# Writing each image's output inside the next image's filter, in four transfers, and asking for the second half of the pixels in the attention's tail

## What is computed

```
q_in = jnp.quantile(x.reshape(B, C, -1), 0.5, axis=-1)        # median of each channel
x = x + relu(-q_in)[:, :, None, None]
y = upfirdn2d(x, lpf, up=2, ...); y = maximum(y, 0); x = upfirdn2d(y, lpf, down=2, ...)
...
spec = rfft2(x); gate = sigmoid(w2 @ gelu(w1 @ abs(spec)))
xf = x + irfft2(spec * gate)
q = xf @ q_w + q_b;  k, v = two strided convolutions of xf, layer norm, projections (320 keys)
out = softmax(q k / 4) v;  out = out @ proj_w + proj_b + x
```

## Time and profile before

| | |
|---|---|
| median of 3 runs | 12392.25 us (12376.9 to 12396.04) |
| profiled execution's own time | 12365.55 us |
| its span, first to last instruction | 12364.0 us |
| mean granted TensorE clock | 0.912 |
| TensorE / VectorE / ScalarE / GpSimd busy | 86% / 72% / 59% / 22% |
| prologue, until the first pass's first TensorE instruction | 257.4 us |
| distance of the 4 MB writes of successive passes, mean of 15 | 756.65 us |

### The profile page before, as it was taken

How to read it: one execution, slowest core, us unless ns; L and a number is a source line. 1 busy time by engine, 2 the same in 40 slices (tenths; PEclk the granted TensorE clock), 3 DMA queues, 4 the chain that set the end, 5 groups by cost and what they waited for, 6 DMA issues and landing times. The chain is left out here.

```text
span 12364.0 us, 195989 instructions
## 1 busy us (share of the span) xinstructions
PE 10662.7 (86%) x71137; PEld 5494.3 (44%) x71137; DVE 8876.6 (72%) x15501; ACT 7240.1 (59%) x12109; POOL 2719.0 (22%) x4368
## 2 busy tenths in 40 slices
PE   2898898989989799898988989889898898979989
PEld 1544435344353443535435354443534435344353
DVE  6777677776677777767677677767777667777776
ACT  5556465664646646466564665646566464664646
POOL 1212213122131221312213121221312213122130
PEclk9899898988989899898998989989898898989989
DMA  1021220212212022130211202112021221202213
GB/s 47 19 48 40 44 60 25 52 29 49 56 29 55 22 52 52 31 71 10 50 48 38 66 19 44 43 42 62 22 52 33 48 57 29 55 22 52 53 30 67
DMA packets 168920, 531.33 MB, mean 43 GB/s; under 512 B 64008, under 2 KB 86536, under 8 KB 153168
## 3 DMA queue, kind: packets, MB, share of 16 engines
q1 hardware_dynamic: 168016, 518.95, 18.7%
HBM read 230.33 MB, written 67.11 MB: 24 GB/s over the span
## 5 line engine op out<-in xcount | busy, mean ns | idle before, releaser
L944 DVE TENSOR_REDUCE R<-ps 128x2 f32<-128x640 f32 x4096 | 3191.7, 817 | 921.7 <-PE ps L681 911.4
L1149 ACT ACTIVATE R<-ps 128x512 f32<-128x512 f32 x5120 | 2820.4, 594 | 645.3 <-PE ps L702 619.7
L248 ACT ACTIVATE R<-R,st 128x1475 bf16<-128x1475 f32 x1326 | 2018.3, 1522 | 854.6 <-DVE st L314 758.5
L302 DVE TENSOR_SCALAR_CACHE_REDUCE R<-R,st 128x1255 bf16<-128x1255 f32 x1326 | 2011.0, 1517 | 20.8
L681 PE MATMUL ps<-KST,R 96*128 96x320 bf16 x8192 | 1875.8, 312 | 67.9 <-DVE R L944 57.6
L727 PE MATMUL ps<-R 128*32 128x512 f32 x12288 | 1635.5, 605 | 38.0 <-DVE Wk L898 32.9
L702 PE MATMUL ps<-R,KST 104*128 104x512 bf16 x4096 | 1576.2, 387 | 21.3 <-ACT R L1149 20.5
L681 PEld LDWEIGHTS ps<-KST,R 96*128 96x128 bf16 x8192 | 761.6, 100 | 830.4 <-DVE R L944 296.5
L1233 POOL CAST R<-Wk 128x512 bf16<-128x512 f32 x256 | 283.8, 1109 | 2931.4 <-DVE Wk L898 2931.4
L702 PEld LDWEIGHTS ps<-R,KST 104*128 104x128 bf16 x4096 | 395.6, 97 | 708.8 <-ACT R L1149 460.6
L203 PE MATMUL ps<-st,cst 128*128 128x6 f32 x884 | 192.3, 289 | 590.5 <-DVE R L302 216.6
(11 more groups left out here) (206 smaller groups left out, 19643.9 us busy)
## 6 DMA issues: line engine op xcount, KB each, us to landing
R<-R SPq DMA_DIRECT2D x3072, 64.0 KB, 2.4
R<-xh_in SPq DMA_DIRECT2D x136, 512.0 KB, 4.4
out_dram<-Z SPq DMA_DIRECT2D x16, 4096.0 KB, 13.2
R<-xa_in SPq DMA_DIRECT2D x36, 1024.0 KB, 11.4
R<-xb_in SPq DMA_DIRECT2D x34, 1024.0 KB, 17.9
R<-sr_in SPq DMA_DIRECT2D x32, 1024.0 KB, 4.8
R<-sr_in SPq DMA_DIRECT2D x16, 2016.0 KB, 9.7
R<-sr_in SPq DMA_DIRECT2D x16, 1056.0 KB
```

The source lines that it names most:

```text
L248: e.activation(junka[:, 0:o2 - o1], xc[:, o1:o2], ACT.Sign, bias=mid, scale=-1.0, accum_out=cnt[:, NP + i:NP + i + 1]).then_inc(md_ca, 1)
L302: e.tensor_scalar(junk[:, 0:o1 - o0], xc[:, o0:o1], mid, None, ALU.is_le, ALU.add, accum_out=cnt[:, i:i + 1]).then_inc(md_cv, 1)
L944: e.tensor_reduce(MX[(4 * u + s4) % 2][:, blk_, h0:h0 + 2], ps[:, 2 + 2 * bq:4 + 2 * bq, 0:320], axis=AX.X, op=ALU.max).then_inc(mx, 1)
L1149: e.activation(PB[:, t % 2, w, :], ps[:, w % 2, :], ACT.Exp).then_inc(ex, 1)
```

## The change

The output of a pass is no longer written at its end. SyncE writes it at the start of the next pass, into the row of the pass that runs (the host rolls the result back by one), in four transfers of 1 MB, quarter q when ScalarE has done its step 2q + 1 (`yr` at 2q + 2). VectorE waits for quarter q's own semaphore before it writes group 4q of Z. After the loop, four transfers write the last image.

The second half of the next pixels is asked for at the end of SyncE's list of a pass, after the last scores (`sc_ps` 320), and the pass's end does not wait for it: its semaphore is not among those cleared there, and VectorE waits for it in the next pass's filter. The two reductions of the first half move into the last block of the attention (t = 31, w = 1 and 4). So the filter has two pieces fewer, and all engines drop the second slot at n = 4 and at n = 8.

In the prologue, VectorE clears Z (the first pass writes it out), waits for both halves before its four reductions, and SyncE loads both halves of the first pass's next image and waits for both.

```diff
-            for _ in range(4):
+            for _ in range(2):
                 yield
...
+        def largest(e, k):
+            e.tensor_reduce(m1[:, k:k + 1], xc[:, 2048 * k:2048 * k + 2048], axis=AX.X, op=ALU.max,
+                            apply_absolute_value=True).then_inc(md_max, 1)
+
+        def dve_median(e, before):
+            for k in (2, 3):
+                if k == 2 and before == 0:
+                    e.wait_ge(in_xc[1], 32)
+                largest(e, k)
                 yield
-            e.wait_ge(md_got, 4)
+            e.wait_ge(md_max, before + 2)
...
-                slot(1 if n >= P or n % 4 == 0 < n else 0)
+                slot(1 if n >= P or n % 4 == 0 and n > 8 else 0)
...
-                    if gq == 0:
-                        e.wait_ge(stored, 16)
+                    if gq % 4 == 0:
+                        e.wait_ge(stored[gq // 4], 16)
...
+                    if t == NT - 1 and w in (1, 4):
+                        e.wait_ge(in_xc[0], 32)
+                        largest(e, w // 4)
...
+        def store(e, row, q):
+            e.dma_start(out[row, :, 2048 * q:2048 * q + 2048].rearrange("a h n -> (a h) n"),
+                        Z[:, 16 * q:16 * q + 16, :].rearrange("p c w -> p (c w)")).then_inc(stored[q], 16)
+
         def sync(e, it):
-            load_next(e, it, 1)
+            for q in range(4):
+                e.wait_ge(yr, 2 * q + 2)
+                store(e, bass.ds(it, 1), q)
...
+            e.sem_clear(in_xc[1])
+            e.wait_ge(sc_ps, 320)
+            load_next(e, it, 1)
             e.wait_ge(in_xc[0], 32)
             e.wait_ge(zo, NT)
-            e.sem_clear(stored)
-            e.dma_start(out[bass.ds(it, 1), :, :].rearrange("a h n -> (a h) n"),
-                        Z[:, :, :].rearrange("p c w -> p (c w)")).then_inc(stored, 16)
...
-            e.memset(st[:, 60:61], 0.0).then_inc(stored, 16)
-            for _ in dve_median(e, in_xc):
+            e.memset(Z[:, :, :], 0.0)
+            for half in range(2):
+                e.wait_ge(in_xc[half], 32)
+            for k in range(2):
+                largest(e, k)
+            for _ in dve_median(e, 2):
                 pass
...
             e.wait_ge(md_end, 1)
-            e.sem_clear(in_xc[0])
-            load_next(e, B - 1, 0)
-            e.wait_ge(in_xc[0], 32)
+            for half in range(2):
+                e.sem_clear(in_xc[half])
+                load_next(e, B - 1, half)
+            for half in range(2):
+                e.wait_ge(in_xc[half], 32)
...
-        nc.sync.wait_ge(stored, 16)
+        for q in range(4):
+            store(nc.sync, slice(0, 1), q)
+        for q in range(4):
+            nc.sync.wait_ge(stored[q], 16)
```

More of the change, by code:

```diff
@@ L154, in program @@
          mx_ps, mx, m8, lay_ps, mr, sc_ps, ex, va_ps, vm, vx, pv_ps, ou, den_ps, rc, on, ot_ps, ox, zb, po_ps, zo,
-         in_w1, in_xc0, in_xc1, in_w20, in_w21, in_w22, in_qs0, in_qs1, in_qs2, in_m0, in_m1,
-         *in_xh, in_c, stored) = signals = [ctx.enter_context(nc.semaphore(n)) for n in SIGNALS]
+         in_w1, in_xc0, in_w20, in_w21, in_w22, in_qs0, in_qs1, in_qs2, in_m0, in_m1,
+         *in_xh, in_c, stored0, stored1, stored2, stored3, in_xc1) = signals = [ctx.enter_context(nc.semaphore(n)) for n in SIGNALS]
+        stored = [stored0, stored1, stored2, stored3]
         zst = [zst0, zst1, zst2, zst3]
@@ L277, in pool_median @@
             yield
-        def dve_median(e, halves):
-            for k in range(4):
-                if halves[k // 2] is not None and k % 2 == 0:
-                    e.wait_ge(halves[k // 2], 32)
-                e.tensor_reduce(m1[:, k:k + 1], xc[:, 2048 * k:2048 * k + 2048], axis=AX.X, op=ALU.max,
-                                apply_absolute_value=True).then_inc(md_got, 1)
+        def largest(e, k):
[6 more added lines that the diff above has]
+                largest(e, k)
                 yield
-            e.wait_ge(md_got, 4)
+            e.wait_ge(md_max, before + 2)
             e.tensor_reduce(pm[:, 0:1], m1, axis=AX.X, op=ALU.max).then_inc(md_v, 1)
@@ L786, in vector @@
         def vector(e):
-            med = dve_median(e, [None, in_xc[1]])
+            med = dve_median(e, 0)
             def slot(n):
@@ L1366, in first_sync @@
             e.wait_ge(md_end, 1)
-            e.sem_clear(in_xc[0])
-            load_next(e, B - 1, 0)
-            e.wait_ge(in_xc[0], 32)
-        cleared = range(signals[0].num, stored.num)
+            for half in range(2):
[3 more added lines that the diff above has]
+                e.wait_ge(in_xc[half], 32)
+        cleared = range(signals[0].num, in_xc1.num)
         with nc.Block() as blk:
```

22 lines of the change are left out of this document (11 added, 11 removed), and 4 rows, old and new, of the table SIGNALS.

## The result

| | before | after |
| --- | --- | --- |
| median, us (4 runs each, same chip) | 12388.45 (12376.9 to 12396.04) | 12242.06 (12240.14 to 12252.08) |
| ratio, 95% interval | | 0.9884 (0.9867 to 0.9901) |
| profiled execution: own time / span, us | 12365.55 / 12364.0 | 12252.08 / 12250.4 |
| TensorE's granted clock | 0.912 | 0.915 |

The changed kernel is faster by 146.4 us between the medians, and by 1.16% by the ratio of the runs; the prediction was 145 us, and 12247 us as a time. The two profiled executions differ by only 113.6 us.

What follows compares the result with a forecast made beforehand. The seam between passes was taken to cost time through the 4 MB write, late instructions and load waits. 2.39 + 4.04 + 3.5 + 0.4 = 10.3 us, 15 times 154.5, less 9.5, gave 145 us: 12247 us, range 12215 to 12315.

Steps and rivals of the forecast that it cites:

- (a): Seam: write leaves, loads are asked for in the tail; saves 2.39 us of load wait and 4.04 us of late instructions.
- (b): Filter: two reductions leave; group 0 comes 2.5 us earlier, the slot at n = 8 gives 1.0 us, together 3.5 us.
- (c): Pass's end: SyncE issues no transfer ahead of the barrier, with the clearing before it 0.4 us saved a pass.
- (d): Attention's last live block: the two moved reductions, 4.56 us, fit an idle stretch of 4.67 us; price 0.
- (e): Filter: four 1 MB writes, about 6 us taken for one, are hidden; price 0, at the upper bound 1.9 us.
- (f): Paid once: prologue 4.5 and 6.4 us, end 2.5 us, less 3.9 us won by the first pass; net 9.5 us.
- the first rival: Seam: late instructions wholly or mostly stay late, so a pass wins 6.3 us, 12307 us; chance 32%.
- at 1009 to 1012 nothing but the instruction packets is left to move: Second pass's start: argument against late instructions staying late; only instruction packets move then, 5 us after the last load.
- The second rival: Filter's first steps: each of four writes holds up an instruction fetch, 1.88 to 3.24 us; slower, 12455 us; chance 6%.
- I take 1.0 us of it: Filter, n = 8: dropping the second slot, which held a 1.52 us count, saves 1.0 us, bounds 0 and 1.6.
- no change: Rival: gains of the early steps are lost to a later wait, as bisection and filter end by other rules; chance 4%.
- the saving is the same on both: Whole run: profiled execution, 12365.55 us, and median of the runs shown, 12392.25 us, were to save the same 145 us.

Runs made afterwards that it cites:

- the pair with idle matmuls: Eight unused matmuls at n = 14 and six at n = 18, added to the kernel before (12336.21 us) and to the changed kernel (12189.69 us).
- the kernel with one transfer of 4 MB: Changed kernel with one 4 MB write at `yr` 2 in place of four of 1 MB: 12238.02 us, ratio 0.9883 to the kernel before.
- the trace with the short prologue: Changed kernel, prologue reducing the first half while the second loads and entering the first pass without waiting for it: 12221.79 us, ratio 0.9877 to the kernel before.
- the kernel with one write: Changed kernel with one 4 MB write for four; two were run, at `yr` 2 (12238.02 us) and at the pass's start (12243.09 us); which is not said.

## Why the prediction came out right

**The total.** 145 us were forecast, 146.4 measured, and the time of 12247 us was 5 us off. The terms, each against what the traces show:

| term | predicted, us | measured, us |
| --- | --- | --- |
| (a) + (b) to group 0, a pass | 2.39 + 4.04 + 2.5 = 8.9 | 29.99 - 21.07 = 8.92 |
| (b) slot at n = 8, a pass | 1.0 | n = 16 comes 9.85 earlier, so 0.9; keeping the slot would have won more, below |
| (c) SyncE ahead of the barrier | 0.4 | 0.3 (last addition to first matmul 2.36, now 2.06) |
| (d) moved reductions | 0 | 0 |
| (e) four writes | 0 | 0 |
| a pass | 10.3 | 10.55; 10.2 without two disturbed passes |
| (f) prologue | 4.5 + 6.4 = 10.9 | 11.9 |
| (f) end | 2.5 | 1.5 |
| (f) first pass | -3.9 | -3.7 |

The row for the slot and those for a pass and the first pass are from the pair with idle matmuls, where only the two falls named above are mixed in (37.89 + 38.87 less 29.56 + 37.35 is 9.85; first passes of 747.37 and 743.63). The whole spans of that pair differ by 151.7 us: 147.7 from the 14 passes, 12.3 from the last pass with the end, 3.7 from the first, less 12.0 from the prologue.

**Late instructions (a).** The first pass was the right model, and the forecast's largest doubt, the first rival with 32%, did not come. Its reason was that loads would be in flight when the jump is made. They were, until about L405 itself, and L469 came at 4.44 us in all 15 later passes. With the loads alone moved the wait stayed, and with 4 MB written just behind the barrier it went: what made the instructions late was the large write that left 2.1 us before L401. My reading of the earlier trace rows was right in that the packets came among the write's, but my case against the first rival took their time as given ("at 1009 to 1012 nothing but the instruction packets is left to move"). Without the write the packet of queue 8 comes 0.47 to 1.05 us after L405, and the loads, which I had expected to be in 1.3 us before it, are in just about then. The forecast stood on the first pass as its model, and that held; this argument for it did not. Every one of those 15 seams has the jump, in the kernel before and in the changed one alike. The Trainium skill (Runtime: NRT & Kernel Launch, "Instruction fetch mechanics") says that a taken branch outside the held blocks forces a fetch before execution goes on. Here the packets are seen at the seam either way, but the stall is seen only with the write, so by these traces the branch alone does not cost the 2 us.

**The second rival**, a fetch behind each write, fell as well: no such wait with four writes in the filter, nor with one of 4 MB there.

**The writes (e).** I took 6 us for 1 MB; it is 3.9. The Trainium skill's fit (SBUF — State Buffer, "The DMA setup-cost knee") gave an estimate of 4.4, nearer than mine; neither changed the sum. What I weighed there as the Trainium skill's case against four transfers came out even: the kernel with one transfer of 4 MB is as fast as that with four.

**The moved reductions (d).** They fit to 0.29 us, as read. The experiment with them alone shows what the cover is: without the earlier loads the same move costs 60 us.

**What failed inside the right sum.** The step "I take 1.0 us of it" for the slot at n = 8 looked one stage ahead only. With clean clocks the slot's removal does win 0.9 us up to n = 16 (38.23 less 37.35), but n = 16 to 24 then takes 1.9 us more (38.26 less 36.36), so in the second pass the kernel with the slot kept is 1.0 us ahead by n = 24 and 0.4 us over the whole pass. And the removal brings the standstills of 1.78 and 1.37 us behind which the clock falls, 32 times in the trace against 7; with those the changed kernel's median is 33 us above that with the slot kept. The prediction had no term for the clock in the middle of the filter at all. It hid in the rival "no change" too: of the 2.4 us by which the first pass was shorter than the seam explained, some 1.4 are falls (an estimate: the first pass has none, the next 14 have 13, 1.5 us each).

**The traced pair.** The step "the saving is the same on both" failed: 113.6 us are traced and 146.4 measured. Of the 33 us, 23 are how far the traced execution of the kernel before lies under its median, and 10 how far that of the changed kernel lies above its own. Falls of the clock would explain both, at about 1.5 us each: the trace of before has 13 (stage 8 to 16 long in 7 passes, 16 to 24 in 6), and its other runs, 11 to 31 us slower, would have some 8 to 19 more; the changed kernel's trace has all 32, and its other runs, 8 to 12 us faster, would have 6 to 8 fewer (the trace with the short prologue has 10 fewer). The 46 us that the idle matmuls win in the kernel before fit, since 30 falls are 45 us, and so does the mean granted clock on record for its unprofiled runs: 0.912 in the profiled run, 0.908 to 0.912 in the others, with 0.912 at 12365.93 us and 0.908 at 12395.28 in one set. But no trace of those runs was taken, and a mean over the run does not say where the clock fell: this part is argued, not shown. The agreement to 1.4 us is in any case partly luck, as the forecast for the two traced executions was 31 us too high. What the clean traces bear out is the saving of a pass, 10.3 us forecast and 10.2 found, and the terms paid once, each to about 1 us.

## What to carry to other kernels

Before a loop's jump, ask what large transfer leaves in the last microseconds ahead of the next pass: a write of the same size started 2 us later, behind the barrier, took away a wait for instructions of 1.9 to 3.2 us in every pass, and the instruction packets' own times showed it. When a change frees an engine earlier, move the data it will ask for next in the same edit; the reductions moved alone made the kernel slower. And find the pass without the suspected cost, here the first one, since its distances gave the saving to a few per cent; then compare stage by stage at equal granted clock before crediting a few microseconds a pass to any part.

## What the runs showed of the hardware that I had not expected

A standstill of 1.78 us is followed by a lower clock in some passes and not in others, with the same instructions around it. TensorE in the second and in the third pass of the kernel with one write:

```profile
1078.60 1.13 PE L469 MATMUL ps<-R,cst 64*128 64x512 f32 x4 [1.78 <-ACT R L1049]
1079.66 1.08 PE L480 MATMUL ps<-R,cst 128*64 128x512 f32 x4
```

```profile
1822.56 1.13 PE L469 MATMUL ps<-R,cst 64*128 64x512 f32 x4 [1.78 <-ACT R L1049]
1823.63 1.88 PE L480 MATMUL ps<-R,cst 128*64 128x512 f32 x4
```

L480 takes 1.08 us in the one and 1.88 in the other. Small shifts of a pass in time can thus win or lose 1.5 us a fall, which is how a kernel that differs in 12 us of prologue can differ by more in its passes. What decides it was not isolated.

Fourteen idle matmuls a pass, 3.6 us of TensorE's time in places where it stood still for 3.15, made the kernel 46 to 52 us faster in 16 passes. A transfer of 4 MB in flight does not by itself hold up instructions: issued 2.1 us before L401 and ahead of the barrier it did, at all 15 seams, for 1.87 to 3.24 us; issued 0.14 to 0.63 us before L405 it did so at none, and issued 10 us behind it at none. Where four pieces of 1 MB began to leave 1.03 to 1.23 us before L405, the wait was only 0.6 to 0.7 us, yet group 0 came some 3 to 4 us later and the clock was low for longer.
